# Shared FFN: one result of the second products is taken out ahead of two operand splits on VectorE

## The reference, cut to what matters

```python
h = x @ w1                      # [8192, 1024] @ [1024, 1024]
x1, x2 = jnp.split(h, 2, axis=-1)
return x1 * jax.nn.silu(x2) @ w2    # [8192, 512] @ [512, 1024]
# outside: x + tanh(g_ffn) * (shared_sum + routed_sum)
```

## Time and profile before

| | us |
|---|---|
| median of three runs | 4186.45 |
| the profiled execution | 4186.12 |
| its span in the trace | 4184.2 |
| shared groups, windows 1 to 5 begin | 2010.7 to 2281.1 |
| window 6 begins | 2353.6 |
| windows 7 to 14 begin | 2419.2 to 2886.9 |

### The profile page before, as it was taken

The page is one execution under the profiler, slowest core; times in us unless marked ns, Lnnn a source line. Parts: engine busy times, 40 slices in busy tenths (PEclk is TensorE's granted clock), DMA queues, the critical chain, the costliest instruction groups (busy, mean ns, idle before and its releaser), DMA issues.

```text
span 4184.2 us, 71612 instructions
## 1 busy us (share of the span) xinstructions
PE 4110.5 (98%) x25930; PEld 3753.8 (90%) x25930; DVE 2504.5 (60%) x2920; ACT 1951.3 (47%) x2580; POOL 1243.3 (30%) x1261
## 2 busy tenths in 40 slices
PE   7999999999999999998999999999999999999997
PEld 7999999999999999997888888888898898888986
DVE  7999999999999999996434422222323323323331
ACT  7888888888888888873111111111212112212120
POOL 2444444444444444431000044440011211111211
PEclk9999999999999999999999999999999999999999
DMA  7888889888898888897232334334434433434432
GB/s 185 221 221 216 222 216 227 216 218 222 216 222 217 227 217 216 221 230 128 76 106 88 93 92 111 107 76 120 121 81 115 105 76 95 109 88 100 89 87 46
DMA packets 279825, 631.72 MB, mean 151 GB/s; under 512 B 45808, under 2 KB 111834, under 8 KB 279702
## 3 DMA queue, kind: packets, MB, share of 16 engines
q1 hardware_dynamic: 218582, 413.89, 32.5%
q0 software_dynamic: 61120, 216.05, 28.4%
HBM read 311.03 MB, written 170.16 MB: 115 GB/s over the span
## 4 chain that ended last, share of the span: by engine, by line
PE 48%; DMA 3%; DVE 1%; issue 1%; ACT 1%; SPq 0%; POOL 0%; DVEq 0%; POOLq 0%; ACTq 0%; PEldq 0%
PE mem_acc L1886 11%; PE mem_acc L1887 11%; PE mem_acc L1888 11%; PE moe_ps L1904 5%; PE moe_ps L1906 4%; PE moe_ps L1905 4%; PE moe_psT L1876 1%; DMA out<-moe_y 1%; DMA moe_y<-out 1%; DMA out<-moe_y,moe_add_i 1%; DVE moe_zl L1786 0%; ACT moe_zh L1560 0%; DVE moe_hid L1799 0%; DVE moe_y L1813 0%; DMA moe_raw<-in_L_ffn_shared_w 0%
## 5 line engine op out<-in xcount | busy, mean ns | idle before, releaser
L1886 PE MATMUL mem_acc<-moe_zh,moe_w1h 128*128 128x512 f32 (+2 forms) x2336 | 848.7, 363 | 12.8 <-issue 7.2
L1887 PE MATMUL mem_acc<-moe_zl,moe_w1h 128*128 128x512 f32 (+2 forms) x2336 | 846.5, 362 | 0.0
L1888 PE MATMUL mem_acc<-moe_zh,moe_w1l 128*128 128x512 f32 (+2 forms) x2336 | 844.2, 361 | 0.0
L900 PE MATMUL mem_acc<-att_kv_hi,att_tz_hi 128*128 128x288 f32 x2560 | 766.2, 299 | 24.6 <-DMA att_tz_lo<-filt_lo 24.6
L902 PE MATMUL mem_acc<-att_kv_hi,att_tz_lo 128*128 128x288 f32 x2560 | 754.9, 295 | 0.0
L901 PE MATMUL mem_acc<-att_kv_lo,att_tz_hi 128*128 128x288 f32 x2560 | 754.7, 295 | 0.0
L1799 DVE TENSOR_TENSOR moe_hid<-mem_acc,moe_act_s 128x512 f32<-128x512 f32 (+2 forms) x148 | 91.6, 619 | 875.2 <-PE mem_acc L1888 837.6
L900 PEld LDWEIGHTS mem_acc<-att_kv_hi,att_tz_hi 128*128 128x128 f32 x2560 | 481.1, 188 | 36.3 <-issue 24.5
L1886 PEld LDWEIGHTS mem_acc<-moe_zh,moe_w1h 128*128 128x128 f32 x2336 | 440.1, 188 | 63.8 <-issue 13.8
L1888 PEld LDWEIGHTS mem_acc<-moe_zh,moe_w1l 128*128 128x128 f32 x2336 | 441.8, 189 | 50.0
L1887 PEld LDWEIGHTS mem_acc<-moe_zl,moe_w1h 128*128 128x128 f32 x2336 | 440.7, 189 | 49.7 <-issue 0.2
(11 more groups left out here) (218 smaller groups left out, 8109.2 us busy)
## 6 DMA issues: line engine op xcount, KB each, us to landing
att_kv_lo<-att_kv POOLq DMA_DIRECT2D x126, 1152.0 KB, 9.7
att_kT<-in_cT SPq DMA_DIRECT2D x64, 512.0 KB, 6.5
att_xn<-in_x SPq DMA_DIRECT2D x64, 512.0 KB, 8.2
out<-att_x SPq DMA_DIRECT2D x64, 512.0 KB, 7.2
z_d<-att_z SPq DMA_DIRECT2D x64, 512.0 KB, 5.9
zT_d<-att_zT SPq DMA_DIRECT2D x64, 512.0 KB, 8.5
moe_y<-out SPq DMA_DIRECT2D x128, 256.0 KB, 4.1
out<-moe_y SPq DMA_DIRECT2D x128, 256.0 KB, 4.9
```

The source lines that it names most:

```text
L900: nc.tensor.matmul(acc, w_hi[:, cols], x_hi, start=start, stop=False, skip_group_check=True)
L1886: nc.tensor.matmul(acc, w1h[j][:, c, b, :], zh[:, c, 0:w], start=(c == 0), stop=False)
L1887: nc.tensor.matmul(acc, w1h[j][:, c, b, :], zl[:, c, 0:w], start=False, stop=False)
L1888: last = nc.tensor.matmul(acc, w1l[j][:, c, b, :], zh[:, c, 0:w], start=False, stop=(c == C - 1))
```

## The change

The first two numbers of `turn_at` for a shared group go from 0 to 1: the splits of tiles 0 and 1 of the next group stand behind the first result instead of ahead of it.

```diff
@@ turn_at(grp, t, halves)
             if halves == 0:
                 return 0
-            return (0, 0, 3, 4)[t] if grp.kind == "shared" else t * halves // grp.nt
+            return (1, 1, 3, 4)[t] if grp.kind == "shared" else t * halves // grp.nt
```

## The result

The changed kernel takes 4195.42 us (median of 20 runs, 4189.93 to 4202.69), the kernel before 4188.9 (median of 20 runs beside it, 4182.92 to 4193.45). The forecast was +7.6 us.

What follows compares the result with a forecast made beforehand. PE was taken as the bound, with late windows ended by the residual's DMA chain. Late windows 7.6, windows 1 to 5 -0.5, window 6 +0.5: +7.6 us on median 4186.45 gives 4194.0, range 4182 to 4200 (8 in 10).

Steps and rivals of the forecast that it cites:

- (a): Shared-group windows except window 6: removing the third half-product's wait for the first result gains 7.2 us gross.
- (b): Windows 7 to 14: splits of tiles 0 and 1 come 0.98 us later, delaying store, residual and PE: +7.6 us.
- The two bounds of (b): Late windows cost 6.6 us if the first result's store landing follows its own request, 7.6 if the z tiles ahead.
- the 0.34 of H2: Each late window: 0.34 us lost where PE's third half-product waits for the first result, 0.23 plus 0.11 for restart.
- (c): Windows 1 to 5: later splits add waits at the seventh half-product against the gain at the third; net -0.5 us.
- (d): Window 6: the first split comes 3.27 us later, delaying the residual and the seventh half-product: +0.5 us.
- (e): VectorE's issue and PE's first products behind each window: no further cost, the +1 us there is hidden.
- The first (faster): Residual in the windows held by traffic, not its request, so the full 7.2 us are gained: 4179; chance 0.12.
- The 0.3 of 0.98 us: Late windows: the change turns to a gain once less than 0.3 of the 0.98 us delay arrives.
- the third rival: Little change: half of the 0.98 us arrives, late windows lose 3.7 us, total 4190; chance 0.15.
- The second, the z tiles: Late windows: the second z tile becomes the bound, one us more in each, 15.6 us slower: 4202; chance 0.13.
- The line of 0.2%: Whole kernel: a measurement tells 0.2% (8.4 us) from no change, bound at 4194.8; slower than that has chance 0.38.

Runs made afterwards that it cites:

- before_again: The kernel before, unchanged, run once more for a second trace; 4193.63 us, ratio 0.9996.
- e1_late: Kernel before with the new VectorE order only in windows 7 to 14; 4192.03 us against 4182.78, ratio 1.0018.
- e2_early: Kernel before with the new VectorE order only in windows 1 to 6; 4183.58 us against 4182.78, ratio 1.0.
- e7_nores_after: Changed kernel without the residual loads of tiles 2 and 3 of each shared group; 4170.17 us, ratio 0.997 to the kernel before.
- e3_store: Changed kernel with SyncE storing the first result ahead of its two z requests; 4173.22 us against 4182.78 for the kernel before, ratio 0.9976.
- e8_sync_only: Kernel before, VectorE's order kept, with SyncE storing the first result ahead of its two z requests; 4197.99 us against 4183.61, ratio 1.0036.
- The dose runs: Kernel before with other VectorE order numbers: (0, 1, 3, 4) ratio 1.0008, (1, 1, 3, 4) ratio 1.0017, (2, 2, 3, 4) ratio 1.014.
- e6_nores_before: Kernel before without the residual loads of tiles 2 and 3 of each shared group; 4176.84 us against 4183.61, ratio 0.9983.
- e5_two: Changed kernel with the splits of tiles 0 and 1 behind the first two results; 4241.41 us against 4183.61 for the kernel before, ratio 1.014.

## Why the prediction was right, point by point

The sums of the window lengths, in us. Old order: traces of the kernel before, before_again, and the windows of e1_late and e2_early that kept it. New order: likewise.

| windows | old order | new order | difference | predicted |
|---|---|---|---|---|
| 1 to 5 | 112.84, 114.39, 114.06 | 112.14, 113.73, 112.70 | -0.9 | -0.5 |
| 6 | 21.91, 21.91, 21.91 | 22.11, 22.39, 23.07 | +0.6 | +0.5 |
| 7 to 14 | 184.04, 192.20, 180.48 | 187.63, 197.98, 192.41 | +7.1 | +7.6 |

**(a) held.** H2 waits in none of the windows with the new order, and 7.2 us gross is what e7_nores_after shows.

**(b) held in mechanism; its sizes did not hold each.** The delay of T0 in windows 9 to 14 is 1.10 us and not 0.98: R0 starts 0.53 us after the start of H0's last matmul (2558.36 against 2557.83), while the 0.42 was read at R1. In the loop the wait for H0 is carried by a register instruction of line 1812, which the trace has at 2558.26, and R0 starts 0.10 us behind it; ahead of R1 it is a plain semaphore instruction. In windows 7 and 8, written out without them, R0 starts after 0.42 and the delay is 1.00. The two bounds of (b) fall together: the store of R0 follows T1's end by 0.89 us as before, since SyncE needs 0.65 us from the second z request to the store, and not 0.52. So the store is requested as much later as the z tiles are, and it doesn't matter which of the two its landing follows. (That the z tiles ahead of it hold it up is seen in e3_store, where it goes first: the residual is requested 3.8 us behind the store in window 1, against 6.0 in the changed kernel.) In the mean of the late windows it goes out 1.0 us later, but PE pays less for it in waits than 0.95 a window. By the distances of starts, its waits in windows 7 to 14 went from 11.8 us (11.1, 16.6, 7.7) to 16.8 (13.3, 20.5, 16.6), 5.0 us or 0.63 a window. (Put the 0.34 of H2 back, and the waits at H5 to H7 are 0.97 us a window longer, where 1.3 was forecast.) The other 2.2 us are a term that the prediction had not at all: stretches behind long waits in which matmuls start every 0.43 us, 0.9 us a trace in the old order (0, 2.6, 0) and 3.1 in the new (1.6, 4.7, 3.0). The sum is right partly because two errors stand against each other, and that part is luck.

Where the rest of the shift goes can be followed in the means of the 24 late windows of either order, from the first matmul of the window:

| us into the window | old order | new order | later by |
|---|---|---|---|
| store of R0 requested | 5.83 | 6.85 | 1.02 |
| first residual requested | 11.98 | 12.73 | 0.75 |
| R4 ends | 16.79 | 17.66 | 0.87 |
| H6 starts | 17.21 | 17.73 | 0.52 |
| H7 starts | 20.60 | 21.36 | 0.76 |

Most of it reaches R4. But (b) took H6 or H7 to be held in every late window. In the old order H6 started right behind R4 in 14 of the 24 windows, H7 right behind R5 in 16, and in 3 windows neither; where they did not, the result had time to spare, and that used up a part of the shift. In the new order H6 starts right behind R4 in 23 of 24, and no window is without a wait. (H7's 0.76 has a part of the slow starts in it.) Whether the 0.27 us between the store and the residual are a faster landing isn't shown: R4's end differs from window to window by 1 us (standard deviation) in either order.

**(c) and (d) held** in the mean, each within 0.4 us of its term, and less well one by one: new waits at H6 in windows 1 to 6 (1.23, 0.38, 0.59, 0.87, 0.73 and 0.19 us in the first trace), T0 0.50 us later in the windows 1 to 4. Window 1 of that trace is 0.42 us longer where 0.17 was forecast, and the old order had waits at H6 too in windows 1 and 4 of other traces, so (c) is no more exact than the traces are alike. In window 6 T0 came 3.27 us later as worked out, but the store of R0 only 2.96 (4.22 to 7.18 us into the window), because it had waited for R0's end before and not for T1's.

Together they make +6.8 us, beside +7.6 forecast and 6.5 between the medians.

**(e) held**: no wait of PE's first products on T3 shows.

**The rivals.** The first (faster) came true when the chain was cut, in e7_nores_after and e3_store, and not here. Its price was wrong, too. If R4 came when it came before, every late window would still end behind the same R4 or R5, as (b) itself says of the upstream 0.34, so only what R4 has to spare in the windows 1 to 5 could be gained: about 3 us, so some 4183 and not 4179 (an estimate: H6 starts there 0.48, 0.74, 0.86, 0.46 and 1.10 us behind R4's end, less 0.05 for the start and 0.11 for the restart each). The 0.3 of 0.98 us at which it was to turn to a gain doesn't follow from its terms either; by the sum of the third rival that point lies near nothing. The gain of 7 us needs R4 to come earlier, as it did in those two runs. The second, the z tiles, is seen in small in this kernel (H5 waits 0.2 and 0.6 us in window 7 of two traces) and in full in e8_sync_only. The third would need half of the shift at PE, and the late windows lost 7.1 us, not 3.7; its condition was nearer than the time tells, since H6 moved by just about half (0.52 us). The dose runs go with a loss that follows the shift: +0.66, +1.1 and +3.7 us at T1 gave +3.4, +7 and +58, or, with the 7.2 gained at H2 put back, about 11, 14 and 65. The line of 0.2% lay, as said, just above the forecast.

## What to carry to other kernels

When PE waits for a result, read on to the wait that ends last in the same stage: here the early one cost 0.3 us a window, and the edit that removed it pushed the DMA chain that ends in the late one. A queue that issues in a fixed order (two loads, then a store) is a dependency too, so an instruction moved on VectorE has to be moved with the transfer that waits for it: VectorE's edit alone cost 7 us, SyncE's alone 14, and both together gained 10. A wait that is slack upstream of a binding one is worth nothing until the binding one is gone, which can be tested by leaving the transfer out, as in e6_nores_before and e7_nores_after.

## What the runs showed of the hardware that was not expected

A long wait can cost PE more than itself. In window 7 of the changed kernel, PE's matmuls at H6, and, with the engines' busy times, the granted clock (the 0.64) of the stretch from 2440 to 2444 us:

```profile
2438.68 0.50 PE L1904 MATMUL moe_ps<-moe_w2h,moe_hh 128*128 128x512 f32 x1 [2.05 <-DVE moe_y L1813]
2439.01 0.39 PE L1905 MATMUL moe_ps<-moe_w2l,moe_hh 128*128 128x512 f32 x1
...
2439.90 0.63 PE L1905 MATMUL moe_ps<-moe_w2l,moe_hh 128*128 128x512 f32 x1
2440.33 0.63 PE L1906 MATMUL moe_ps<-moe_w2h,moe_hl 128*128 128x512 f32 x1
...
2443.12 0.39 PE L1904 MATMUL moe_ps<-moe_w2h,moe_hh 128*128 128x512 f32 x1
```

```profile
2440.00:2444.00 4.00, 4.00 (x13) 3.15 (x12) 1.43 (x2) 0.00 (x0) 2.06 (x6) 0.64 0.35 90
```

The engine had been idle for 2.05 us; 0.8 us after it started again its matmuls came every 0.43 us for eight starts. The granted clock was 0.50 from 2440 to 2442 us, the lower of its two levels (1.2 GHz), 0.64 in the mean of 2440 to 2444, and 1.00 again from 2443: 1.6 us on top of the wait. Not every such wait is followed by it; the one of 2.33 us in window 9 of the same trace (2574.15) is not. In the kernel before repeated, one followed a wait of 3.2 us:

```profile
2847.53 0.79 PE L1904 MATMUL moe_ps<-moe_w2h,moe_hh 128*128 128x512 f32 x1 [3.20 <-DVE moe_y L1813]
2848.13 0.63 PE L1905 MATMUL moe_ps<-moe_w2l,moe_hh 128*128 128x512 f32 x1
```

For an exchange of many short waits for few long ones, as this change is, that is a price of its own, 2.2 us here and 13.4 in e5_two.

The second is that a load takes longer with a store ahead of it. The first z tile of a window landed 3.6 us after its request in window 1 of the kernel before, 4.7 us in e3_store (one store of 256 KB ahead of it and under way) and 5.1 in e8_sync_only, where the first z request goes out 1 us after the store. The medians of all 54 loads of z tiles between 2000 and 2990 us are 5.1, 5.4 and 5.9 us. The kernels differ in when these loads go out as well, so how much of it is the store's isn't shown.
